# Rotary attention in a twelve-stage decoder: values projected in two halves, keys added by VectorE, the mask ahead of the normalising

## What is computed

```python
qkv = x @ W_qkv                                   # x: layer-normalised, (32, 64, 128); W_qkv: (128, 3 * 1024)
q, k, v = to_heads of the three parts             # 16 heads of 64
q, k = t * cos + rotate_half(t) * sin             # rotary positions
dots = einsum('bhid,bhjd->bhij', q, k) * 64 ** -0.5
attn = softmax(where(causal, neg, dots))
out = einsum('bhij,bhjd->bhid', attn, v)          # back to (32, 64, 1024)
out = relu(out @ W_o1) @ W_o2
out = (out - mean) * rsqrt(var + 1e-05) * gamma   # and x = x + out
```

## Time and profile before

| | |
|---|---|
| device time, median of 3 runs | 1715.52 us (1708.34 to 1720.39) |
| the profiled execution | 1705.7 us, span 1703.9 us, mean granted TensorE clock 0.792 |
| busy over the span: TensorE, weight loads, VectorE, ScalarE, GpSimd | 69%, 52%, 62%, 37%, 39% |
| the stage of the change in the span | about 368 us (first transposes) to 619 us (first matmul of the next stage) |

### The profile page before, as it was taken

How to read it: one execution, slowest core, us unless ns; L and a number is a source line. 1 busy time by engine, 2 the same in 40 slices (tenths; PEclk the granted TensorE clock), 3 DMA queues, 4 the chain that set the end, 5 groups by cost and what they waited for, 6 DMA issues and landing times. The chain is left out here.

```text
span 1703.9 us, 35618 instructions
## 1 busy us (share of the span) xinstructions
PE 1175.2 (69%) x14040; PEld 891.6 (52%) x14040; DVE 1064.7 (62%) x2853; ACT 627.9 (37%) x1475; POOL 667.4 (39%) x726
## 2 busy tenths in 40 slices
PE   7982438927888769654566853199938884776778
PEld 5652337816767646543244643178815551563556
DVE  4989601156899938833666598333449947856672
ACT  2641213305666646211544331012205433543343
POOL 3447444433555535443123224723333424324320
PEclk9985569968999979767677765599969856877878
DMA  8900136540000058021000100245410000000000
GB/s 269 141 2 2 42 113 177 162 137 2 3 3 3 3 85 119 3 82 64 0 1 1 26 1 1 101 134 170 158 50 1 2 1 1 1 2 1 1 2 26
DMA packets 72010, 89.13 MB, mean 52 GB/s; under 512 B 5823, under 2 KB 59138, under 8 KB 71200
## 3 DMA queue, kind: packets, MB, share of 16 engines
q1 hardware_dynamic: 65824, 76.89, 17.9%
q0 software_dynamic: 6016, 9.93, 1.7%
HBM read 56.55 MB, written 32.69 MB: 52 GB/s over the span
## 5 line engine op out<-in xcount | busy, mean ns | idle before, releaser
L757 POOL TENSOR_TENSOR arena<-arena,small 128x1024 f32<-128x1024 f32 x80 | 154.0, 1930 | 132.6 <-ACT arena L639 87.4
L372 POOL TENSOR_SCALAR var_eps<-moments 128x1 f32<-128x1 f32 (+1 forms) x136 | 37.1, 273 | 335.9 <-DVE moments L365 335.8
L687 ACT ACTIVATE arena<-arena 128x1024 f32<-128x1024 f32 x80 | 84.6, 1058 | 132.2 <-DVE arena L831 132.2
L554 PE MATMUL ps<-arena,q 64*64 64x512 f32 x640 | 102.6, 715 | 37.5 <-issue 20.6
L2079 POOL TENSOR_TENSOR arena<-arena 128x512 f32<-128x512 f32 x64 | 79.9, 1282 | 103.5 <-DVE arena L2097 103.5
L564 PEld LDWEIGHTS ps<-small,arena 128*128 128x128 f32 x640 | 80.7, 157 | 71.4 <-issue 37.2
L564 PE MATMUL ps<-small,arena 128*128 128x128 f32 x640 | 99.3, 305 | 12.3 <-ACT arena L687 10.6
L1598 PEld LDWEIGHTS ps<-expert_ring,arena 128*128 128x128 f32 (+1 forms) x864 | 104.5, 192 | 2.9
L712 ACT COPY arena<-ps 128x512 f32<-128x512 f32 x160 | 87.1, 588 | 50.4 <-PE ps L564 49.7
L1598 PE MATMUL ps<-expert_ring,arena 128*128 128x128 f32 (+1 forms) x864 | 104.7, 275 | 0.0
L374 POOL TENSOR_TENSOR rstd<-var_eps,minus_half 128x1 f32<-128x1 f32 (+1 forms) x136 | 99.8, 734 | 11.3
(11 more groups left out here) (359 smaller groups left out, 2922.6 us busy)
## 6 DMA issues: line engine op xcount, KB each, us to landing
expert_ring<-L2f_in SPq DMA_DIRECT2D x23, 704.0 KB, 4.2
expert_ring<-L0f_in SPq DMA_DIRECT2D x23, 578.0 KB, 3.9
slots_L0f<-blank SPq DMA_DIRECT2D x1, 8385.0 KB, 50.0
slots_L2f<-blank SPq DMA_DIRECT2D x1, 8385.0 KB, 50.3
small<-small_in SPq DMA_DIRECT2D x1, 4231.5 KB, 19.0
expert_ring<-L1f_in SPq DMA_DIRECT2D x8, 512.0 KB, 3.9
arena<-slots_L0f SPq DMA_DIRECT2D x23, 129.0 KB, 3.1
arena<-slots_L2f SPq DMA_DIRECT2D x23, 129.0 KB, 3.5
```

Of the source, the lines that this page charges most:

```text
L554: last = pe.matmul(c.ps[part(b), m], c.q[part(m), at:at + S], kx(t)[part(m), b * 512:(b + 1) * 512], start=True, stop=True)
L687: act.activation(buf(k), buf(k), ACT.Exp, scale=exp_scale).then_inc(s.probs_ready, 1)
L757: g.tensor_tensor(kx(t).rearrange("p (b h k) -> p b h k", b=2, k=S), bcast(of_tile, 2, HEADS // 2), bcast(bcast(c.w("head_of_row"), 2, S), ...
```

## The change

In the loops of this one stage:

- TensorE projects the values of a tile one step earlier, in two halves of 512 columns: the first between weighing and output projection, the second at the end of the step, behind the scores and the second matrix (while VectorE adds the mask). Turning the weights moves between query and key projection.
- VectorE adds the two halves of the keys itself (`add_turned_keys`, new), behind the rotation; GpSimd keeps the queries' adds. The wait for the products is one on VectorE's own semaphores.
- VectorE normalises a tile one step later, right behind the mask of the next tile and ahead of that one's maxima; it did so at the end of the step before, ahead of the mask.
- Scale, gamma and the sum into x become two `scalar_tensor_tensor`: (att - mean) * gamma, and that * rstd + x.
- ScalarE's 16 exponentials of a tile lie 5, 6 and 5 around the copies of the weighed values and the rectifying (8, 4 and 4 before), all behind the copy of the turned weights, and signal once, behind the last.
- GpSimd inverts for the following norm ahead of the stage's own.

The diff, cut to the loops and what they call (ScalarE's copies are the old ones, moved into functions):

```diff
-            def project_values(t):
+            def project_values(t, half):
                 if t == 1 or t == 2:
                     pe.wait_ge(s.v_ready, t)
                 elif t >= 3:
                     pe.wait_ge(s.probsT_ready, 2 * (t - 2))
-                for m in range(2):
-                    last = pe.matmul(c.ps[:, 4 + m], c.hT[:, tok(t)],
-                                     w[:, 2 * INNER + m * 512:2 * INNER + (m + 1) * 512], start=True, stop=True)
-                last.then_inc(s.v_ps, 1)
+                at = 2 * INNER + half * 512
+                pe.matmul(c.ps[:, 4 + half], c.hT[:, tok(t)], w[:, at:at + 512], start=True, stop=True)\
+                    .then_inc(s.v_ps, 1)
...
+            project_values(0, 0)
+            project_values(0, 1)
             for t in range(NT + 2):
                 if t < NT:
-                    project_values(t)
                     project(t, 0)
+                if t >= 2:
+                    turn_probs(t - 2)
+                if t < NT:
                     project(t, 1)
                 if t >= 2:
-                    turn_probs(t - 2)
                     weigh_values(t - 2)
+                if t + 1 < NT:
+                    project_values(t + 1, 0)
+                if t >= 2:
                     project_out(t - 2)
                 if t < NT:
                     scores(t)
                 if t >= 2:
                     project_mid(t - 2)
+                if t + 1 < NT:
+                    project_values(t + 1, 1)
...
             for k in range(NT + 3):
                 if 0 <= k - 3 < NT:
...
+                    take_mid(k - 3)
                 if k < NT:
...
+                    take_values(k)
+                if 0 <= k - 2 < NT:
+                    take_turned_probs(k - 2)
+                if 0 <= k - 1 < NT:
+                    soften(k - 1, range(5))
+                if 0 <= k - 2 < NT:
+                    take_weighed(k - 2)
+                if 0 <= k - 1 < NT:
+                    soften(k - 1, range(5, 11))
+                if 0 <= k - 2 < NT:
+                    rectify(k - 2)
+                if 0 <= k - 1 < NT:
+                    soften(k - 1, range(11, 16))
...
             for k in range(NT + 6):
+                if 0 <= k - 5 < NT:
+                    invert(c, g, following, k - 5)
                 if 0 <= k - 4 < NT:
                     invert(c, g, own, k - 4)
                 if k < NT:
-                    for i, signal in enumerate((s.q_rotated, s.k_rotated)):
-                        g.wait_ge(s.by_sin, 2 * k + i + 1)
-                        for half in range(2):
-                            own_half = rotated[i][:, half * 512:(half + 1) * 512]
-                            g.tensor_tensor(own_half, own_half, sines[i][:, (1 - half) * 512:(2 - half) * 512], ALU.add)\
-                                .then_inc(signal, 1)
-                if 0 <= k - 5 < NT:
-                    invert(c, g, following, k - 5)
+                    g.wait_ge(s.by_sin, 2 * k + 1)
+                    for half in range(2):
+                        own_half = rotated[0][:, half * 512:(half + 1) * 512]
+                        g.tensor_tensor(own_half, own_half, sines[0][:, (1 - half) * 512:(2 - half) * 512], ALU.add)\
+                            .then_inc(s.q_rotated, 1)
...
+            def add_turned_keys(t):
+                v.wait_ge(s.by_cos, 2 * t + 2)
+                v.wait_ge(s.by_sin, 2 * t + 2)
+                for half in range(2):
+                    own_half = rotated[1][:, half * 512:(half + 1) * 512]
+                    v.tensor_tensor(own_half, own_half, sines[1][:, (1 - half) * 512:(2 - half) * 512], ALU.add)\
+                        .then_inc(s.k_rotated, 1)
...
             for k in range(NT + 6):
-                softened = 0 <= k - 1 < NT
-                if softened:
+                if 0 <= k - 1 < NT:
                     mask(k - 1)
+                if 0 <= k - 2 < NT:
+                    normalise(k - 2)
+                if 0 <= k - 1 < NT:
                     find_max(k - 1)
                 if k < NT:
                     rotate(k, 0)
                     rotate(k, 1)
+                    add_turned_keys(k)
                 t = k - 4
                 if 0 <= t < NT:
-                    scale(v, own, c.att, c.hn, t)
-                    v.wait_ge(own.normed, t + 1)
-                    v.tensor_tensor(c.hn[:, t], c.hn[:, t], c.w("L1_gamma"), ALU.mult).then_inc(s.weighted, 1)
+                    v.wait_ge(own.rstd, t + 1)
+                    v.scalar_tensor_tensor(out=c.hn[:, t], in0=c.att[:, t], scalar=own.moments_of[:, t, 0:1],
+                                           in1=c.w("L1_gamma"), op0=ALU.subtract, op1=ALU.mult).then_inc(s.weighted, 1)
                     v.wait_ge(s.weighted, t + 1)
-                    v.tensor_tensor(c.x[:, t], c.x[:, t], c.hn[:, t], ALU.add).then_inc(s.added, 1)
+                    v.scalar_tensor_tensor(out=c.x[:, t], in0=c.hn[:, t], scalar=own.rstd_of[:, t:t + 1],
+                                           in1=c.x[:, t], op0=ALU.mult, op1=ALU.add).then_inc(s.added, 1)
...
-                if softened:
-                    normalise(k - 1)
```

More of the change, by code:

```diff
@@ L2022, in soften @@
             def soften(t, groups):
+                act.wait_ge(s.bias_ready, t + 1)
                 for g in groups:
@@ L2027, in soften, with take_mid, take_values, take_turned_probs @@
                                           accum_out=c.row_max[:, t, g:g + 1])
-                last.then_inc(s.exp_ready, 1)
+                if groups[-1] == HEADS - 1:
+                    last.then_inc(s.exp_ready, 1)
+            def take_mid(t):
+                act.wait_ge(s.y_ps, t + 1)
+                act.copy(c.att[:, t], c.ps[:, 7, 0:P]).then_inc(s.y_ready, 1)
+            def take_values(t):
+                act.wait_ge(s.v_ps, 2 * t + 2)
+                if t >= 3:
+                    act.wait_ge(s.o_ps, t - 2)
+                act.copy(values(t), c.ps[:, 4:6].rearrange("p b n -> p (b n)")).then_inc(s.v_ready, 1)
+            def take_turned_probs(t):
+                for j in range(2):
+                    act.wait_ge(s.probsT_ps, 2 * t + j + 1)
+                    if t > 0:
+                        act.wait_ge(s.o_ps, t)
+                    act.copy(probsT[:, j * 512:(j + 1) * 512], c.ps[:, 4 + j]).then_inc(s.probsT_ready, 1)
+            def take_weighed(t):
+                act.wait_ge(s.o_ps, t + 1)
+                if t > 0:
+                    act.wait_ge(s.mid_ps, t)
+                for b in range(2):
+                    act.copy(outT[:, b * 512:(b + 1) * 512], c.ps[:, 6 + b]).then_inc(s.o_ready, 1)
+            def rectify(t):
+                act.wait_ge(s.mid_ps, t + 1)
+                act.activation(c.oT[:, tok(t)], c.ps[:, 6, 0:P], ACT.Relu).then_inc(s.mid_ready, 1)
             for q in range(QUARTERS):
@@ L2034, in _ @@
                 if 0 <= k - 3 < NT:
-                    act.wait_ge(s.y_ps, k - 2)
-                    act.copy(c.att[:, k - 3], c.ps[:, 7, 0:P]).then_inc(s.y_ready, 1)
+                    take_mid(k - 3)
                 if k < NT:
-                    act.wait_ge(s.v_ps, k + 1)
-                    if k >= 3:
-                        act.wait_ge(s.o_ps, k - 2)
-                    act.copy(values(k), c.ps[:, 4:6].rearrange("p b n -> p (b n)")).then_inc(s.v_ready, 1)
-                newer = 0 <= k - 1 < NT
-                if newer:
-                    act.wait_ge(s.bias_ready, k)
-                    soften(k - 1, range(8))
-                t = k - 2
-                if not 0 <= t < NT:
-                    if newer:
-                        soften(k - 1, range(8, 16))
-                    continue
-                for j in range(2):
-                    act.wait_ge(s.probsT_ps, 2 * t + j + 1)
-                    if t > 0:
-                        act.wait_ge(s.o_ps, t)
-                    act.copy(probsT[:, j * 512:(j + 1) * 512], c.ps[:, 4 + j]).then_inc(s.probsT_ready, 1)
-                if newer:
-                    soften(k - 1, range(8, 12))
-                act.wait_ge(s.o_ps, t + 1)
-                if t > 0:
-                    act.wait_ge(s.mid_ps, t)
-                for b in range(2):
-                    act.copy(outT[:, b * 512:(b + 1) * 512], c.ps[:, 6 + b]).then_inc(s.o_ready, 1)
-                if newer:
-                    soften(k - 1, range(12, 16))
-                act.wait_ge(s.mid_ps, t + 1)
-                act.activation(c.oT[:, tok(t)], c.ps[:, 6, 0:P], ACT.Relu).then_inc(s.mid_ready, 1)
+                    take_values(k)
[11 more added lines that the diff above has]
+                    soften(k - 1, range(11, 16))
         @block.gpsimd
@@ L2116, in normalise @@
                 shaped = by_position(probs(t))
[L2117 removed]
+                v.wait_ge(s.exp_ready, t + 1)
                 v.reciprocal(c.row_inv[:, t], c.row_max[:, t]).then_inc(s.inv_ready, 1)
```

2 lines of the change are left out of this document (removed).

## The result

The changed kernel takes **1687.01 us** (median of 4 runs, 1682.51 to 1697.83), the kernel before 1711.93 (median of 4 runs beside it, 1707.48 to 1720.39): a ratio of 0.985 with a 95% interval of 0.981 to 0.9895, so faster by more than 1%. The prediction was 1690 us, 1678 to 1705. The profiled execution after took 1688.84 us, its span is 1687.0.

A forecast was written before the change was run, and what follows sets the result against it. The bound was a loop of mask, projection, rotation, GpSimd's four adds and scores; VectorE would set 12.1 us steps. Fill 5, steady 21.6 and drain -1 gain 25.6 us, so 1690 us against 1715.52, range 1678 to 1705.

The forecast's parts named there:

- TensorE's way round: Steady step on TensorE, from scores through mask, projections, turning, weighing and output to the next scores: 11.95 us.
- VectorE's sum: VectorE's work in one steady step, adding the keys itself, with fused unblocked products: 12.05 to 12.3 us, 12.1 taken.
- the walk: VectorE's new step followed row by row: key products end at 10.22, then adds, fused products and the rest, 12.05 us.
- Keys ready: VectorE's two key adds, 0.65 us each plus 0.33 waiting for GpSimd, end 11.85 us after the scores start.
- Products freed: VectorE's two fused 128x128 products run unblocked by GpSimd at 0.31 us each; the 1.91 us lost per step is gone.
- Softening: ScalarE's last five exponentials end by about 2.1 us, VectorE's reciprocal comes at 2.78: no cost, 0.65 us to spare.
- The start: Stage fill to mask 2: first scores 1.2 us earlier, mask 0 to 2 about 24.5 us from 28.36; 5 us gained.
- The end: Drain from mask 15 to the last h: last exponentials wait for the output projection, 1 us lost.
- A: Rival: VectorE's reciprocal waits for late exponentials; if 1.5 us late, step 12.95, 1701 us; chance 0.13.
- B: Rival: VectorE becomes the bound, key adds 1.25 us each, step 13.0, 1702 us; chance 0.13.
- C: Rival: GpSimd's query adds and VectorE's key adds take turns, keys at 14.06 us or later, 1716 to 1721; chance 0.06.
- D: Rival: TensorE's granted clock falls, a step 5 to 9 us longer, 1780 us if all 13 steps; chance 0.03.

The follow-up runs named there:

- the keys alone: Kernel before, with only the key adds moved from GpSimd to VectorE: steps 13.24 us but for three of 14.7 to 14.8; launch 1711.43 us against 1715.85.
- the unfused experiment: Changed kernel with scale, gamma and the sum into x as three instructions again: steps 12.01 to 12.02 us from 442.58 on; launch 1686.58 us against 1725.52.
- normalising first: Changed kernel with VectorE normalising the older tile ahead of the newer tile's mask again: step 13.75 us; launch 1711.94 us against 1727.17 of before.
- the early exponentials: Changed kernel with all eleven remaining exponentials of the last tile ahead of the rectifying: launch 1690.73 us, ratio to before 0.986 (0.979 to 0.992).
- the mask alone: Kernel before, with only normalising moved behind the next tile's mask: step 13.75 us, one of 15.29; launch 1724.35 us against 1715.85.

## Why the prediction was right

**TensorE's way round: right.** 11.95 was forecast, 11.89 measured, and leaving work out showed that this round sets the step. Its parts hold too: from the scores through the mask to the query projection 2.91 (2.89 forecast), from the weighing through the copies to the output 2.36 (2.36); the turning, 0.87 from start to start, makes most of the difference. The waits of 0.1 and 0.25 that the sum has in these two are there, at 0.20 and 0.41, though no row shows them, since a half of the values takes 0.86 and not 0.94.

**VectorE's sum: too long.** 12.05 to 12.3 was forecast, and the step of 12.1 taken from it; 11.78 is what VectorE takes where TensorE doesn't hold it. Half of the 0.27 against the walk is in the key adds, put at 1.63 with their wait for GpSimd: from the end of line 2114 they take 479.09 - 477.61 = 1.48. The wait is as forecast (GpSimd ends at 475.43 + 2.50 = 477.93, 0.32 behind the products), but the two adds then take 1.16 and not 1.30. The rest is 0.06 ahead of the adds and some 0.08 behind the fused products. So the engine named as the bound was the wrong one, by 0.1 to 0.2 us; the steady part gained 24.3 in place of 21.6.

**Keys ready: right in kind.** Forecast 11.85, behind the scores' start, and TensorE at 11.95. Measured 479.09 - 467.45 = 11.64 (the scores of that step start at 479.34 - 11.89 = 467.45), and TensorE at 11.89. 0.62 us is an unblocked add, against the 0.65 taken.

**What held the step before: misread in part.** The prediction has GpSimd's adds hold TensorE, as the scores start 0.24 us behind the last add, and puts them into the loop. But that row shows no wait, and the scores start 1.98 behind the output's start (477.86 to 479.84 in the earlier trace rows), exactly as after (477.36 to 479.34). The adds held VectorE, through the two blocked products, and VectorE held the mask, and with it the next query projection. Without the blocking (the keys alone) VectorE waits for TensorE, and the step is TensorE's 13.24. The forecast of the new step doesn't rest on that reading: it walks the new order.

**Products freed: right, and so the rule of exclusion.** 0.34 and 0.35 against 0.31 forecast. The Trainium skill (SBUF — State Buffer, section Who interferes with whom) has VectorE work with two SBUF inputs and GpSimd work that reads SBUF exclude each other. The trace agrees on both sides: 1.24 us with four adds on GpSimd, 0.29 to 0.35 with two. The rule spoke against an add on VectorE, but the place decided: the adds fell where GpSimd had just finished.

**Softening: right in the steady part.** The reciprocal never waits there, and the exponentials end near 481.4, 0.7 us ahead of the reciprocal at 482.11, as the 0.65 of the forecast.

**The start: wrong.** 5 us were forecast, 1.0 measured. Relative to the projections the first scores come earlier as forecast (wait of 5.76 before, 4.47 from the end of the projections after, 1.29 gained against 1.2). What failed is the term for the clock, 0.5 us. From the first transposes to mask 0 the granted clock is 0.68 after, against 0.79 before, and the values of tile 0 take 3.78 where they took 1.98:

```profile
380.87 3.78 PE L1951 MATMUL ps<-L_qkv,hT 128*128 128x512 f32 x4 [0.68 <-ACT hT L2067]
```

Where the clock is up, the forecast holds: in the unfused experiment, which has the changed kernel's work up to mask 2, these values take 1.98 at a granted clock of 0.81, mask 0 comes 16.6 us behind the transposes and mask 2 24.4 behind that, 5.0 less than before in all. Whether the change has a part in the lower clock stays open. TensorE's work up to these values is the same in every kernel, and of the nine experiments on the changed kernel three (GpSimd adding the keys, normalising first, unfused) have them at 1.98; but six have 3.7 to 3.8 like the changed kernel, and none of the three traces with the old order (before, and its two parts) does.

**The end: wrong.** 1 us was charged, 4.8 lost. The mechanism (exponentials behind the output projection) was right and worth 2.2. The other term, the lower clock for tile 15's own work, was left out.

**The sum.** Steady 24.3, start 1.0, end -4.8 make 20.4 in this pair, against 25.6; the medians give 24.9. The misses of the start and the end, 4.0 and 3.8, are made up in part by the steps, 2.7 better. That the medians come within 1 us of the forecast gain is luck: in this pair the stage gained 5 us less, and the launches of either kernel spread over 13 to 15 us.

**The rivals.** A (reciprocal waits) happens when normalising is put first, and in the drain, never in the steady part. B came nowhere as described: in the changed kernel the two adds are 1.37 together; VectorE is the bound only where it adds the queries too, and there an add takes 0.62. C came nowhere: the query adds start behind the query products. D holds at the two ends only; the steady part of the changed kernel has 1.00.

## What to carry to other kernels

When two engines wait for each other, write down every loop with its length, not only the busiest engine: here loops of 13.17 us (GpSimd's four adds ahead of the scores), 13.24 (TensorE's old order) and 13.75 (the normalising ahead of the mask, or exponentials ahead of the copies that TensorE wants) lay beneath the 13.80, and the two parts made alone gained 0.56 and 0.05 us where the whole gained 1.91. A product of two SBUF tiles on VectorE can take four times as long beside GpSimd's adds (1.24 us against 0.29), so look for rows far above their own price elsewhere and clear the other engine's queue rather than the instruction. An engine without a bracketed wait need not be the bound, and can still wait: compare the distance of two starts with the same work back to back. An order that suits the steady part should be walked through the last round too, where an engine that waits early holds up what stands behind it.

## What was not expected of the hardware

**The clock in the drain.** After, the granted clock is 0.50 from 581 to 603 us (the 1.2 GHz level) although TensorE is busy 15.0 of 22 us there. Before, it fell too (0.61 from 594 to 607 us), but came back:

```profile
607.00:614.00 7.00, 4.71 (x92) 4.13 (x92) 2.28 (x9) 2.69 (x6) 1.56 (x4) 1.00 0.01 2
```

So the output projection of tile 15 takes 3.78 us after, and 2.05 before (at 611.26). Before, tile 15's turning follows tile 14's second matrix without idle time, behind which the clock is at 1.00; after, TensorE waits 2.49 us there for the normalising. In the run with the early exponentials that wait is 0.33, and the clock is 0.52 all the same. Whether the waits decide it stays open.

**Short falls of the clock in the steady part.** The changed kernel's trace has none, but other runs do. With the keys alone three output projections take 3.65 to 3.68 us in place of 2.05; the granted clock is 0.57 from 445 to 449 us, where the first of them is, and 1.00 on both sides. With the mask alone there is one such stretch (0.60 from 559 to 563), and in the kernel without the fused products and half the output projection a query projection of 3.61 (0.57 from 532 to 536). They lengthen a step by 1.4 to 1.6 us; what brings them on is open.

**Pauses of TensorE with nothing to wait for.** In the kernel with half the output projection, three steps are 12.8 to 13.9 us, by breaks in TensorE's work, as here within the scores:

```profile
514.84 0.37 PE L1964 MATMUL ps<-arena 32*64 32x64 f32 x15 [1.83 <-issue]
```

1.83 us pass after the 113th of 128 matmuls without a releaser in the profile. In two further steps it is 1.76 us, seven matmuls before the end of the scores, and 1.34 us ahead of the values. The kernel without the fused products as well has its three breaks (2.11, 1.76 and 1.34 us) at the same matmuls, so it is hardly the chance of one execution. The changed kernel has none in its steady part. The cause is open; it wasn't tried.
